# A linear-attention and expert layer on one core: the order of steps inside the token blocks is changed

## The chip, the core and the metric

The kernel runs on one core of a Trainium2 chip. The metric is the time of one execution on the device in microseconds (us); of several runs the median is taken. The engines named here are PE (TensorE), DVE (VectorE), ACT (ScalarE), POOL (GpSimd) and SP (SyncE, which here issues most DMAs).

## The reference

The input is x with 2 x 8192 tokens of 512 values. Two parts are added to it in turn.

```python
x = x + attention(layernorm(x))      # 16 heads of 32, chunks of 64 tokens
x = x + experts(layernorm(x))        # 64 experts, top 8, 256 places each, and a shared one

# attention: q, k, v are projections; alpha = 0.9 * sigmoid(silu(x Wg1 + bg1) Wg2 + bg2) + 0.1
scores = einsum('bhncd,bhnkd->bhnck', qc, kc) / sqrt(D)   # inside a chunk, causal
intra  = einsum('bhnck,bhnke->bhnce', softmax(scores), vc)
def step(S, inp):                                         # one token after the other
    q_t, k_t, v_t, a_t = inp
    inter_t = einsum('bhd,bhde->bhe', q_t, S)
    return a_t[..., None] * S + k_t[..., None] * v_t[..., None, :], inter_t
# experts: softmax of the router's logits, the best 8, their weights normed; an expert takes
# its first 256 tokens; silu(x Wg) * (x Wu) Wd; the shared expert has 384 hidden values
```

## The kernel before

There are two stages. `phase_tokens` goes through 64 blocks of 256 tokens and writes the attention's output with the shared expert added (`out_dram`), the normed rows with their router weights (`norm_rows`), and the counts of tokens by expert. `phase_experts` then goes through the 64 experts; the change does not touch it.

Every engine has its own program, and semaphores tie them together. In `phase_tokens` an engine's program is a loop over `step(t)`, where `t` is a block, `n` the next one and `m` the one after that. A step is a list of calls written out by hand, and that list is the order in which the engine works; an engine that has to wait holds all that stands behind. PE's steps work on three blocks at once: the end of block `t` (its last scores and outputs, the shared expert), the projections and first scores of `n`, and the transposes, the gate and half of the query projection of `m`. PE's loop body holds 16 steps and is run three times, then 14 steps follow written out, and a tail for the last two blocks.

What PE does in a block falls into two kinds.

Large products (`split_product`, L802 to L804): each product of float values is made of three, high by high, high by low, low by high. `project` makes keys and queries (12 products of 256 columns for each quarter, called a part), `values` and `down` have 512 columns, `gate_up` makes 24 products for each third of the hidden values.

Small products: `scores(t, u)` (four a block) has decayed keys by decayed queries (`inter`, L901) and queries by keys (`intra`, L915), one for each head and chunk. `outputs(t, u)` (four a block) has probabilities by values (L960) and the state by decayed queries (L972). `state_updates(t, odd)` (L881) has keys by values for the state, first the even chunks, then the odd ones; the second call waits for the first one's last product (`dk_filled`). The profile has two records for each of these products and one for each large one. So `scores` is 96 records of products, `outputs` 64, and `state_updates` 64, each with as many weight loads.

Between them stand transposes: `xt` (L819), `ktok` (L861), `turn_probs` (L938), `turn_out` (L983), `x2t` (L993), `turn_logits` (L1019).

Four of the eight banks of PSUM are shared by 23 jobs of PE. The table `JOBS` names for each job its bank and, in the order of its rows, what came in the bank before it; `take` (L790) lets PE wait for the reader of the last tenant.

POOL makes the inverse products (`unpair`, L494 and L496), folds them, and multiplies keys (`decayed_k`, L529) and queries (`decayed_q`, L521). `scores(n, 0)` waits for both, `ktok` for the keys. `rstd2(t, k)` (L473) gives DVE the factor that `norm2` waits for.

DVE reads scores and outputs from PSUM, makes the softmax, and has the scans of the decays (`decays`, L1278), the routing (`route_a`, `route_b`, `route_rows`), the state (`state`, chunk by chunk) and the sums. SP waits in a fixed order (L396 to L406): for both `x2_ready`, then it loads X of the block after next; for `rows_ready` (from `route_rows`), then it stores the normed rows; for `out_ready` (from `total`), then it stores the output; for the counts, then it stores these.

Of the kernel before, what the change touches and what calls it, by code (L numbers as in the profile page):

```python
# [135 lines left out]
def phase_tokens(nc, x_rows, Wq, bq, Wk, bk, Wv, bv, Wg1, bg1, Wg2, bg2, router_w, ws_gate_up,  # L136
                 ws_down, out_rows, norm_rows, counts_dram, ends_dram):
    ctx = ExitStack()
    with ctx:
# [284 lines left out]
        def _(pool):  # L424
# [123 lines left out]
            fold(Turn(0, 63))  # L548
            decayed_k(Turn(0, 63))
            decayed_q(Turn(0, 63))  # L550
# [5 lines left out]
        def _(act):  # L556
# [116 lines left out]
            def q_evac(t, k):  # L673

                qk_evac(t, k, q_filled, q_ready, QT, bq4s, SCALE, ("Qa", "Qb"))
# [5 lines left out]
            def step(t):  # L681
                n = t.next()
                m = t.next(2)
                q_evac(n, 0)
                gate2(n, 0)
# [27 lines left out]
                gate1(m)  # L713
                exp(n, 1)
                s1_high(m)
# [4 lines left out]
            gate1(Turn(0, 0))  # L720
            s1_high(Turn(0, 0))
            q_evac(Turn(0, 0), 0)
# [9 lines left out]
            exp(Turn(0, 0), 0)  # L732
            xt_evac(Turn(0, 1), 0)
            xt_evac(Turn(0, 1), 1)
            gate1(Turn(0, 1))
            exp(Turn(0, 0), 1)
            s1_high(Turn(0, 1))
# [3 lines left out]
            q_evac(Turn(0, 63), 0)  # L741
            gate2(Turn(0, 63), 0)
# [15 lines left out]
            ktok_evac(Turn(0, 63), 0)  # L758
            router_exp(Turn(0, 62))
            ktok_evac(Turn(0, 63), 1)  # L760
            hidden_high(Turn(0, 62), 0)
            gu(Turn(0, 62), 1)
            exp(Turn(0, 63), 0)
            hidden_high(Turn(0, 62), 1)
            gu(Turn(0, 62), 2)
            hidden_high(Turn(0, 62), 2)
# [20 lines left out]
        def _(pe):  # L787
# [1295 lines left out]
```

## Time and profile before

| what | us |
|---|---|
| median of 3 runs | 4517.09 |
| lowest and highest run | 4503.93, 4520.61 |
| the profiled execution, whole | 4525.55 |
| its span, first to last instruction | 4523.8 |
| PE busy | 4300.5 (95%) |
| PE weight loads busy | 3867.9 (86%) |
| DVE busy | 3486.0 (77%) |
| ACT busy | 2285.8 (51%) |
| POOL busy | 1326.0 (29%) |
| mean granted clock of PE | 0.967 |

The page is of one execution. Weight loads lie beside products, so both can be busy at once. Matmuls are pipelined and their ends are modelled: how far apart products start tells more than how long one takes. A clock of 1.00 is 2.4 GHz, 0.50 is 1.2 GHz. "issue" as a releaser means that the engine stood although nothing that the profile shows held it. The token stage fills the first 3565 us, the experts the rest.

### The profile page before, as it was taken

Reading aid. Unit: us, or ns where it says so; the run is one execution under the profiler, and the core shown is the slowest. Engines: PE = TensorE matmul, PEld = TensorE weight load, DVE = VectorE, ACT = ScalarE, POOL = GpSimd, SP = SyncE. Lnnn points to the kernel's source line nnn. Section 1 sums busy time; section 2 is a strip of 40 time slices with the busy share of each in tenths; the row PEclk is TensorE's granted clock in tenths of the full one; section 3 lists DMA queues with packets and bytes.
Section 4 is the critical chain, followed back from the end, with each engine's and each line's share of the span. In section 5 each row is a group of like instructions: output and inputs, shape, how many; then the busy total and the mean of one; then the engine's idle time right before and its main releaser. Section 6 shows DMA issues by size and latency. Waiting matters only on the chain. (4 is left out here: it accounts for less than half of the span.)

```text
span 4523.8 us, 182121 instructions
## 1 busy us (share of the span) xinstructions
PE 4300.5 (95%) x73868; PEld 3867.9 (86%) x73868; DVE 3486.0 (77%) x7674; ACT 2285.8 (51%) x7515; POOL 1326.0 (29%) x1266
## 2 busy tenths in 40 slices
PE   5999999999999999999999999999999689999998
PEld 4888888888888888888888888888888579999998
DVE  5777777777777777777777777777777588888887
ACT  4444444444445444444444444545444256666665
POOL 1222222222222222222222222222222156666665
PEclk9999999999999999999999999999999789999999
DMA  2010000000001001001011000110110179999997
GB/s 65 33 36 32 32 32 32 32 32 32 32 32 42 32 32 32 32 32 32 32 37 32 32 32 32 32 32 32 38 37 32 71 235 265 269 265 269 269 265 194
DMA packets 195679, 357.32 MB, mean 79 GB/s; under 512 B 17856, under 2 KB 94016, under 8 KB 194992
## 3 DMA queue, kind: packets, MB, share of 16 engines
q1 hardware_dynamic: 161488, 268.55, 17.7%
q0 software_dynamic: 33632, 79.73, 7.8%
q8 instruction: 544, 8.91, 0.8%
q14 instruction: 15, 0.12, 0.0%
HBM read 242.95 MB, written 107.50 MB: 77 GB/s over the span
## 5 line engine op out<-in xcount | busy, mean ns | idle before, releaser
L473 POOL TENSOR_TENSOR rs<-ve,neg_half 128x1 f32<-128x1 f32 x128 | 78.5, 614 | 2537.1 <-DVE ve L1377 2536.9
L618 ACT ACTIVATE PR<-PR,MX 128x64 f32<-128x64 f32 x2048 | 680.6, 337 | 2.0 <-DVE MX L1336 1.7
L802 PE MATMUL bank<-XBh,wsguh 128*128 128x256 f32 x1536 | 442.0, 288 | 1.5 <-DVE WG L1448 1.5
L626 ACT ACTIVATE OTs<-ot_bank 128x256 f32<-128x256 f32 x256 | 98.4, 384 | 677.6 <-PE ot_bank L960 677.4
L1936 PE MATMUL ebank<-XH,WH 128*128 128x256 f32 x1536 | 430.7, 280 | 7.6 <-DVE XL L2018 7.6
L803 PE MATMUL bank<-XBl,wsguh 128*128 128x256 f32 x1536 | 430.8, 280 | 0.0
L804 PE MATMUL bank<-XBh,wsgul 128*128 128x256 f32 x1536 | 430.8, 280 | 0.0
L1936 PE MATMUL ebank<-XH,WL 128*128 128x256 f32 x1536 | 429.6, 280 | 0.0
L1936 PE MATMUL ebank<-XL,WH 128*128 128x256 f32 x1536 | 429.6, 280 | 0.0
L618 ACT ACTIVATION_READ_ACCUMULATOR PR<-PR,MX 128x1 f32 x2048 | 389.6, 190 | 0.0
L2011 DVE TENSOR_TENSOR WL<-WS,WH 128x768 fp32r<-128x768 f32 (+1 forms) x455 | 370.9, 839 | 16.2
L802 PE MATMUL bank<-XTh,wkh 128*128 128x256 f32 x1024 | 338.9, 331 | 1.6 <-issue 1.1
L1873 ACT ACTIVATE WH<-WS 128x768 fp32r<-128x768 f32 (+1 forms) x455 | 325.2, 747 | 28.1 <-DMA WS<-in_L_ffn_w_down_dram 28.1
L803 PE MATMUL bank<-XTl,wkh 128*128 128x256 f32 x1024 | 312.5, 305 | 2.6 <-issue 2.6
L804 PE MATMUL bank<-XTh,wkl 128*128 128x256 f32 x1024 | 311.8, 304 | 2.0 <-issue 2.0
L802 PE MATMUL bank<-XTh,wqh 128*128 128x256 f32 x1024 | 299.3, 292 | 0.0
L1936 PEld LDWEIGHTS ebank<-XH,WH 128*128 128x128 f32 x1536 | 289.4, 188 | 11.1 <-issue 8.0
L802 PEld LDWEIGHTS bank<-XBh,wsguh 128*128 128x128 f32 x1536 | 290.0, 189 | 1.7 <-DVE WG L1448 1.6
L1936 PEld LDWEIGHTS ebank<-XL,WH 128*128 128x128 f32 x1536 | 288.6, 188 | 2.1
L803 PEld LDWEIGHTS bank<-XBl,wsguh 128*128 128x128 f32 x1536 | 290.3, 189 | 0.0
L804 PEld LDWEIGHTS bank<-XBh,wsgul 128*128 128x128 f32 x1536 | 289.9, 189 | 0.0
L1936 PEld LDWEIGHTS ebank<-XH,WL 128*128 128x128 f32 x1536 | 289.5, 189 | 0.0
(231 smaller groups left out, 13341.0 us busy)
## 6 DMA issues: line engine op xcount, KB each, us to landing
WS<-in_L_ffn_w_gate_dram SPq DMA_DIRECT2D x65, 768.0 KB
WS<-in_L_ffn_w_up_dram SPq DMA_DIRECT2D x65, 768.0 KB
WS<-in_L_ffn_w_down_dram SPq DMA_DIRECT2D x65, 768.0 KB
norm_rows<-XR SPq DMA_DIRECT2D x64, 576.0 KB, 3.9
X<-in_L_attn_x_dram SPq DMA_DIRECT2D x64, 512.0 KB, 3.6
out_dram<-X SPq DMA_DIRECT2D x64, 512.0 KB, 5.1
CR<-token_counts,count_at POOLq DMA_INDIRECT x136
XG<-norm_rows,row_at POOLq DMA_INDIRECT x132
```

The source lines that it names most:

```text
L473: nc.gpsimd.tensor_tensor(rs2[:, k:k + 1], ve2[:, k:k + 1], neg_half[:, k:k + 1], ALU.pow).then_inc(rstd2_ready.sem, 1)
L618: ins = nc.scalar.activation(PR[b][:, j, :], PR[b][:, j, :], ACT.Exp, bias=MX[b][:, j:j + 1], scale=1.0, accum_out=SU[b][:, j:j + 1])
L626: nc.scalar.activation(OTs[u // 2][:, 2 * (u % 2):2 * (u % 2) + 2, :], ot_bank[:, 0:2 * P].rearrange("p (a b) -> p a b", a=2), ACT.Copy).t ...
L802: nc.tensor.matmul(out, sh, mh, start=first, stop=False)
L803: nc.tensor.matmul(out, sh, ml, start=False, stop=False)
L804: return nc.tensor.matmul(out, sl, mh, start=False, stop=last)
L1873: nc.scalar.activation(WH[t.buf][:, cols], WS[t.buf][:, cols], ACT.Copy).then_inc(wh_ready.sem, 1)
L1936: last = nc.tensor.matmul(bank[HID[m]][:, a * CAP:(a + 1) * CAP], w, x[odd][:, c, :], start=(c == 0 and i == 0), stop=(c == KC - 1 and i = ...
L2011: v.tensor_tensor(WL[t.buf][:, cols], WS[t.buf][:, cols], WH[t.buf][:, cols].bitcast(f32), ALU.subtract).then_inc(wl_ready.sem, 1)
```

## The change

Only orders are changed, and with them the table of banks. On PE: `outputs(t, 0)` moves from behind `turn_probs(t, 1)` to the step before, between pieces of `down`; `scores(n, 2)` and the gate products move up; `scores(t, 3)` opens the step; halves of the key projection stand behind it and behind `outputs(t, 1)`; the two halves of the state products are parted by `xt`, the turn of the normed rows; `scores(n, 0)` comes ahead of `ktok(n, 0)`; some pieces of `values`, of the query projection and of `x2t` are joined. On POOL the queries come ahead of the keys and `unpair` ahead of `rstd2(t, 0)`. On ACT and DVE some 20 steps move by a few places; on DVE `route_rows` goes ahead of `scores_part(n, 1)`, the scans move from the head of a step to the end of the one before, ahead of `total(t, 1)`, and `state` is called in three pieces where it was two. The opening and the tail, written out by hand, are changed in the same way.

```diff
 JOBS = {
-    "Ka": (2, 1), "Kb": (0, 1), "ATr0": (1, 0), "Qb": (3, 1), "V0": (1, 1), "V1": (0, 1), "ATr1": (2, 0), "X2Ta": (3, 0),
-    "X2Tb": (2, 0), "RL": (3, 0), "GU0": (2, 0), "RLT": (3, 0), "KTok0": (0, 1), "KTok1": (0, 1), "GU1": (2, 0), "DK": (0, 1),
...
+    "Ka": (2, 1), "ATr0": (1, 0), "Kb": (0, 1), "Qb": (3, 1), "V0": (1, 1), "ATr1": (2, 0), "V1": (0, 1), "X2Ta": (3, 0),
+    "X2Tb": (2, 0), "RL": (3, 0), "GU0": (1, 0), "RLT": (3, 0), "KTok0": (2, 1), "KTok1": (3, 1), "GU1": (0, 0), "DK": (1, 1),
...
             def step(t):
                 n = t.next()
                 fold(t)
+                decayed_q(t)
                 decayed_k(t)
-                decayed_q(t)
                 rstd1(n)
+                unpair(n)
                 rstd2(t, 0)
-                unpair(n)
                 rstd2(t, 1)
 
             rstd1(Turn(0, 0))
...
             def step(t):
                 n = t.next()
                 m = t.next(2)
-                q_evac(n, 0)
-                gate2(n, 0)
                 gate2(n, 1)
                 alpha(n)
                 ot(t, 0)
@@ -699,27 +697,29 @@
                 lt(t)
                 gu(t, 0)
                 ktok_evac(n, 0)
+                ktok_evac(n, 1)
                 router_exp(t)
-                ktok_evac(n, 1)
+                hidden_high(t, 0)
                 normalise(m)
-                hidden_high(t, 0)
                 gu(t, 1)
+                xt_evac(m, 0)
+                hidden_high(t, 1)
+                xt_evac(m, 1)
+                gu(t, 2)
                 exp(n, 0)
-                xt_evac(m, 0)
-                xt_evac(m, 1)
-                hidden_high(t, 1)
-                gu(t, 2)
+                gate1(m)
                 hidden_high(t, 2)
-                gate1(m)
+                q_evac(m, 0)
+                s1_high(m)
                 exp(n, 1)
-                s1_high(m)
+                gate2(m, 0)
 
...
             def step(t):
                 n = t.next()
                 m = t.next(2)
-                turn_probs(t, 1)
+                scores(t, 3)
                 project(n, 0, wk, k_filled, ("Ka", "Kb"), parts=(0,))
-                outputs(t, 0)
-                scores(t, 3)
                 outputs(t, 1)
-                project(n, 1, wk, k_filled, ("Ka", "Kb"), parts=(0,))
-                turn_out(t, 0)
                 project(n, 0, wk, k_filled, ("Ka", "Kb"), parts=(1,))
                 turn_probs(t, 2)
-                project(n, 1, wk, k_filled, ("Ka", "Kb"), parts=(1,))
+                turn_out(t, 0)
+                project(n, 1, wk, k_filled, ("Ka", "Kb"), parts=(0,))
+                project(n, 1, wq, q_filled, ("Qa", "Qb"), parts=(0,))
                 outputs(t, 2)
                 turn_probs(t, 3)
-                project(n, 1, wq, q_filled, ("Qa", "Qb"), parts=(0,))
+                project(n, 1, wk, k_filled, ("Ka", "Kb"), parts=(1,))
+                outputs(t, 3)
                 values(n, 0, chunks=(0,))
-                outputs(t, 3)
-                values(n, 1, chunks=(0,))
                 turn_out(t, 1)
-                values(n, 1, chunks=(1,))
                 project(n, 1, wq, q_filled, ("Qa", "Qb"), parts=(1,))
+                values(n, 1, chunks=(0, 1))
                 values(n, 0, chunks=(1, 2))
                 x2t(t, 0)
+                x2t(t, 1)
                 values(n, 1, chunks=(2,))
-                x2t(t, 1)
                 values(n, 0, chunks=(3,))
                 values(n, 1, chunks=(3,))
                 router_high(t)
                 router_low(t)
                 gate_up(t, 0)
                 turn_logits(t)
+                scores(n, 0)
                 ktok(n, 0)
-                scores(n, 0)
                 ktok(n, 1)
                 gate_up(t, 1)
                 state_updates(n, 0)
-                state_updates(n, 1)
                 xt(m, 0)
                 xt(m, 1)
+                state_updates(n, 1)
+                positions(t)
                 gate_up(t, 2)
                 scores(n, 1)
-                positions(t)
                 gate1(m)
-                turn_probs(n, 0)
                 project(m, 0, wq, q_filled, ("Qa", "Qb"))
                 down(t, 0, (0, 1))
+                turn_probs(n, 0)
+                scores(n, 2)
+                gate2(m, 0)
+                gate2(m, 1)
                 down(t, 0, (2,))
+                outputs(n, 0)
                 down(t, 1, (0, 1))
                 down(t, 1, (2,))
-                gate2(m, 0)
-                gate2(m, 1)
-                scores(n, 2)
+                turn_probs(n, 1)
 
...
             def step(t):
                 n = t.next()
                 m = t.next(2)
-                decays(n)
-                scores_part(t, 3)
                 softmax_b(t, 2)
                 products(n)
+                decay_part(t, 3)
+                weights(t, 2)
                 residual(t, 0)
-                weights(t, 2)
-                decay_part(t, 3)
                 softmax_b(t, 3)
+                inverse(n, 0)
+                weights(t, 3)
+                inverse(n, 1)
                 variance2(t, 0)
-                weights(t, 3)
-                inverse(n, 0)
-                inverse(n, 1)
                 residual(t, 1)
                 variance2(t, 1)
                 norm2(t, 0)
...
                 route_b(t)
                 hidden_low(t, 0)
                 hidden(t, 1)
-                state(n, (0,))
                 xt_low(m, 0)
+                state(n, (0, 1))
                 xt_low(m, 1)
+                route_rows(t)
+                scores_part(n, 1)
                 hidden_low(t, 1)
                 hidden(t, 2)
+                state(n, (2,))
+                silu1(m)
                 softmax_b(n, 0)
-                scores_part(n, 1)
-                state(n, (1, 2, 3))
-                silu1(m)
+                decay_part(n, 1)
+                state(n, (3,))
                 hidden_low(t, 2)
+                s1_low(m)
                 route_c(t)
-                decay_part(n, 1)
                 weights(n, 0)
+                scores_part(n, 2)
+                decay_part(n, 2)
                 total(t, 0)
-                s1_low(m)
                 softmax_b(n, 1)
-                route_rows(t)
+                decays(m)
+                weights(n, 1)
                 total(t, 1)
-                scores_part(n, 2)
-                weights(n, 1)
-                decay_part(n, 2)
+                scores_part(n, 3)
 
...
```

What follows are rows of the built programs, PE first, of one block in the middle of PE's loop, without register instructions where dots stand. A row names line, operation, written and read tiles, the size and how many follow each other; one small product here is two records in the profile. First PE before, from the first outputs of a block to its second ones (L960 and L972 are `outputs`, L901 and L915 `scores`):

```order
L960 MATMUL ot_bank<-WT,V 32x64 x8
L972 MATMUL ot_bank<-QD,R 32x64 x16
L960 MATMUL ot_bank<-WT,V 32x64 x8
L901 MATMUL sa<-QD,RI 32x64 x2
...
L915 MATMUL sa<-KT,QT 64x64 x16
...
L901 MATMUL sa<-QD,RI 32x32 x2
L960 MATMUL ot_bank<-WT,V 32x64 x8
L972 MATMUL ot_bank<-QD,R 32x64 x16
```

PE after, from the first outputs of a block to its second ones (`wsd` is the shared expert's second matrix, `wk` the keys'):

```order
L835 MATMUL bank<-sg,wg 128x256 x2
L802 MATMUL bank<-wsdh,HTh 128x512
L803 MATMUL bank<-wsdl,HTh 128x512
L804 MATMUL bank<-wsdh,HTl 128x512
L960 MATMUL ot_bank<-WT,V 32x64 x8
L972 MATMUL ot_bank<-QD,R 32x64 x16
...
L938 MATMUL pt_bank<-ident,PR 128x128 x4
L901 MATMUL sa<-QD,RI 32x64 x2
...
L915 MATMUL sa<-KT,QT 64x64 x16
...
L802 MATMUL bank<-XTh,wkh 128x256
...
L960 MATMUL ot_bank<-WT,V 32x64 x8
```

First outputs, fourth scores and second outputs stood in one run; now three blocks of large products, 3, 9 and 12, lie ahead of each of the three.

PE before, at the state products (L881) and the turn of the normed rows of the block after (L819):

```order
L804 MATMUL bank<-XBh,wsgul 128x256
L881 MATMUL bank<-V,KTok 32x32 x64
...
L819 MATMUL sa<-ident,XN 128x128 x4
L819 MATMUL pt_bank<-ident,XN 128x128 x4
L802 MATMUL bank<-XBh,wsguh 128x256
```

PE after, at the same place (L1028 is `positions`):

```order
L881 MATMUL bank<-V,KTok 32x32 x32
...
L819 MATMUL sa<-ident,XN 128x128 x4
L819 MATMUL pt_bank<-ident,XN 128x128 x4
L881 MATMUL bank<-V,KTok 32x32 x32
L1028 MATMUL ot_bank<-upto,M 64x256
```

The eight transposes went between the halves, and `positions` came up behind them.

POOL before, one step (L502 to L510 fold, L469 is `rstd1`, L473 `rstd2`):

```order
L510 TENSOR_TENSOR AL<-AL,r_mid 128x16x32
...
L529 TENSOR_TENSOR RI<-KT,RI 128x1024
L518 REGISTER_ALU
L521 TENSOR_TENSOR QD<-QT,AL 128x1024
L468 REGISTER_ALU
L469 TENSOR_TENSOR rs<-ve,neg_half 128x2
L472 REGISTER_ALU
L473 TENSOR_TENSOR rs<-ve,neg_half 128x1
L492 REGISTER_ALU
L494 TENSOR_TENSOR RI<-PV,AL 128x32x16
L496 TENSOR_TENSOR RI<-PV,AL 128x32x16
```

POOL after, the same step:

```order
L521 TENSOR_TENSOR QD<-QT,AL 128x1024
L527 REGISTER_ALU
L529 TENSOR_TENSOR RI<-KT,RI 128x1024
L468 REGISTER_ALU
L469 TENSOR_TENSOR rs<-ve,neg_half 128x2
L492 REGISTER_ALU
L494 TENSOR_TENSOR RI<-PV,AL 128x32x16
L496 TENSOR_TENSOR RI<-PV,AL 128x32x16
L472 REGISTER_ALU
L473 TENSOR_TENSOR rs<-ve,neg_half 128x1 x2
```

Queries and keys changed places, and both calls of `rstd2` now stand behind `unpair`.

## Rows read from the trace of the kernel before

**Rows 1.** The page: busy time, share of the span and instructions of each engine.
```profile
PE 4300.5 (95%) x73868; PEld 3867.9 (86%) x73868; DVE 3486.0 (77%) x7674; ACT 2285.8 (51%) x7515; POOL 1326.0 (29%) x1266
```

**Rows 2.** Line 835 in the token stage: duration least/median/most, first and last start.
```profile
L835 PE MATMUL bank<-sg,wg x252: 274/280/356, 89.8 to 3494.8; 128*128 128x256 f32 x126
```

**Rows 3.** Stretches of one block: length, busy time of engines, clock, DMA share, GB/s.
```profile
2181.33:2236.22 54.89, 53.72 (x1058) 47.70 (x1057) 42.11 (x97) 26.36 (x100) 11.23 (x10) 0.97 0.09 33
2236.22:2292.77 56.55, 54.49 (x1058) 48.54 (x1057) 42.07 (x97) 26.34 (x100) 11.48 (x10) 0.94 0.10 32
2791.40:2844.00 52.60, 52.07 (x1058) 46.22 (x1058) 42.12 (x97) 26.35 (x100) 11.50 (x10) 1.00 0.10 34
...
3331.10:3383.80 52.70, 52.19 (x1058) 46.32 (x1058) 42.17 (x97) 26.36 (x100) 11.51 (x10) 1.00 0.10 34
```

**Rows 4.** Waits of PE, 140 to 3440: line, releaser, us in total, times, longest.
```profile
PE ot_bank L960 <- issue: 25.5, 18, 2.9
PE sa L901 <- issue: 18.3, 15, 1.6
PE bank L881 <- PE bank L881: 16.2, 60, 0.4
PE ot_bank L972 <- issue: 13.9, 10, 1.8
PE sa L915 <- issue: 7.8, 12, 0.9
PE pt_bank L938 <- issue: 6.9, 2, 3.7
```

**Rows 5.** Timeline of PE: start, duration, instructions; in brackets the idle time before.
```profile
2238.99 0.28 PE L802 MATMUL bank<-XTh,wkh 128*128 128x256 f32 x1
2239.11 0.28 PE L803 MATMUL bank<-XTl,wkh 128*128 128x256 f32 x1
...
2241.44 0.44 PE L901 MATMUL sa<-QD,RI 32*32 32x64 f32 x32
2241.80 0.69 PE L915 MATMUL sa<-KT,QT 32*64 32x64 f32 x32
...
2245.35 0.85 PE L972 MATMUL ot_bank<-QD,R 32*32 32x64 f32 x21 [1.79 <-issue]
...
2247.10 0.41 PE L803 MATMUL bank<-XTl,wkh 128*128 128x256 f32 x1
2247.31 0.41 PE L804 MATMUL bank<-XTh,wkl 128*128 128x256 f32 x1
```

**Rows 6.** A stretch with its DMA share; a store's issue on SP; the instruction queue.
```profile
2238.60:2242.40 3.80, 3.80 (x142) 3.26 (x140) 3.77 (x7) 1.54 (x5) 0.00 (x0) 1.00 0.80 296
...
2238.29 1.80 SPq L404 DMA_DIRECT2D out_dram<-X  x1
...
q8 instruction: 544, 8.91, 0.8%
```

**Rows 7.** A stretch behind the stall.
```profile
2244.80:2246.00 1.20, 0.65 (x21) 0.61 (x20) 1.17 (x5) 0.00 (x0) 0.00 (x0) 0.50 0.00 0
```

**Rows 8.** The first of three long stretches of the token stage.
```profile
189.00:1279.00 1090.00, 1056.20 (x20822) 939.50 (x20822) 832.05 (x1891) 519.25 (x1973) 224.78 (x199) 0.97 0.10 33
```

**Rows 9.** Timeline of DVE at the scans.
```profile
2240.87 2.49 DVE L1278 TENSOR_TENSOR_SCAN AL<-AL,seg_start 128x264 f32<-128x264 f32 x4
```

**Rows 10.** Timeline of PE at the state products.
```profile
2220.68 0.68 PE L881 MATMUL bank<-V,KTok 64*32 64x32 f32 x56 [0.27 <-PE bank L881]
...
2221.81 0.63 PE L819 MATMUL sa<-ident,XN 128*128 128x128 f32 x4
```

**Rows 11.** Timeline of POOL at the queries.
```profile
2211.20 2.22 POOL L521 TENSOR_TENSOR QD<-QT,AL 128x1024 f32<-128x1024 f32 x1
```

**Rows 12.** Timeline of PE at the first scores.
```profile
2214.32 0.61 PE L861 MATMUL bank<-ident,RI 128*128 128x128 f32 x4
2214.86 0.44 PE L901 MATMUL sa<-QD,RI 32*32 32x64 f32 x32
```

More of the change, by code:

```diff
@@ L720, in _ @@
             gate1(Turn(0, 0))
+            q_evac(Turn(0, 0), 0)
             s1_high(Turn(0, 0))
-            q_evac(Turn(0, 0), 0)
             gate2(Turn(0, 0), 0)
@@ L1128, in _ @@
             values(Turn(0, 0), 1, chunks=(3,))
+            scores(Turn(0, 0), 0)
             ktok(Turn(0, 0), 0)
-            scores(Turn(0, 0), 0)
             ktok(Turn(0, 0), 1)
             state_updates(Turn(0, 0), 0)
-            state_updates(Turn(0, 0), 1)
             xt(Turn(0, 1), 0)
             xt(Turn(0, 1), 1)
+            state_updates(Turn(0, 0), 1)
             scores(Turn(0, 0), 1)
             gate1(Turn(0, 1))
+            project(Turn(0, 1), 0, wq, q_filled, ("Qa", "Qb"))
             turn_probs(Turn(0, 0), 0)
-            project(Turn(0, 1), 0, wq, q_filled, ("Qa", "Qb"))
+            scores(Turn(0, 0), 2)
             gate2(Turn(0, 1), 0)
             gate2(Turn(0, 1), 1)
-            scores(Turn(0, 0), 2)
+            outputs(Turn(0, 0), 0)
+            turn_probs(Turn(0, 0), 1)
             with nc.Fori(0, 24, 8, engines=[pe.engine], hint_back_edge=True) as pair:
@@ L1176, in _ @@
             turn_logits(Turn(0, 62))
+            scores(Turn(0, 63), 0)
             ktok(Turn(0, 63), 0)
-            scores(Turn(0, 63), 0)
             ktok(Turn(0, 63), 1)
@@ L1182, in _ @@
             state_updates(Turn(0, 63), 1)
+            positions(Turn(0, 62))
             gate_up(Turn(0, 62), 2)
             scores(Turn(0, 63), 1)
-            positions(Turn(0, 62))
+            down(Turn(0, 62), 0, (0, 1))
             turn_probs(Turn(0, 63), 0)
-            down(Turn(0, 62), 0, (0, 1))
+            scores(Turn(0, 63), 2)
             down(Turn(0, 62), 0, (2,))
+            outputs(Turn(0, 63), 0)
             down(Turn(0, 62), 1, (0, 1))
             down(Turn(0, 62), 1, (2,))
-            scores(Turn(0, 63), 2)
             turn_probs(Turn(0, 63), 1)
-            outputs(Turn(0, 63), 0)
             scores(Turn(0, 63), 3)
             outputs(Turn(0, 63), 1)
+            turn_probs(Turn(0, 63), 2)
             turn_out(Turn(0, 63), 0)
-            turn_probs(Turn(0, 63), 2)
             outputs(Turn(0, 63), 2)
@@ L1208, in _ @@
             gate_up(Turn(0, 63), 1)
+            positions(Turn(0, 63))
             gate_up(Turn(0, 63), 2)
-            positions(Turn(0, 63))
             down(Turn(0, 63), 0, (0, 1))
@@ L1548, in _ @@
             decay_part(Turn(0, 0), 0)
-            state(Turn(0, 0), (0,))
             xt_low(Turn(0, 1), 0)
+            state(Turn(0, 0), (0, 1))
             xt_low(Turn(0, 1), 1)
+            scores_part(Turn(0, 0), 1)
+            state(Turn(0, 0), (2,))
+            silu1(Turn(0, 1))
             softmax_b(Turn(0, 0), 0)
-            scores_part(Turn(0, 0), 1)
-            state(Turn(0, 0), (1, 2, 3))
-            silu1(Turn(0, 1))
             decay_part(Turn(0, 0), 1)
+            state(Turn(0, 0), (3,))
+            s1_low(Turn(0, 1))
             weights(Turn(0, 0), 0)
-            s1_low(Turn(0, 1))
+            scores_part(Turn(0, 0), 2)
+            decay_part(Turn(0, 0), 2)
             softmax_b(Turn(0, 0), 1)
-            scores_part(Turn(0, 0), 2)
+            decays(Turn(0, 1))
             weights(Turn(0, 0), 1)
-            decay_part(Turn(0, 0), 2)
+            scores_part(Turn(0, 0), 3)
             START = links[0]
@@ L1569, in _ @@
             links[0], links[1] = START + 62 * LINKS, None
-            decays(Turn(0, 63))
-            scores_part(Turn(0, 62), 3)
             softmax_b(Turn(0, 62), 2)
             products(Turn(0, 63))
+            decay_part(Turn(0, 62), 3)
+            weights(Turn(0, 62), 2)
             residual(Turn(0, 62), 0)
-            weights(Turn(0, 62), 2)
-            decay_part(Turn(0, 62), 3)
             softmax_b(Turn(0, 62), 3)
+            inverse(Turn(0, 63), 0)
+            weights(Turn(0, 62), 3)
+            inverse(Turn(0, 63), 1)
             variance2(Turn(0, 62), 0)
-            weights(Turn(0, 62), 3)
-            inverse(Turn(0, 63), 0)
-            inverse(Turn(0, 63), 1)
             residual(Turn(0, 62), 1)
@@ L1632, in _ @@
             hidden(Turn(0, 63), 1)
+            route_rows(Turn(0, 63))
             hidden_low(Turn(0, 63), 1)
@@ L1637, in _ @@
             total(Turn(0, 63), 0)
-            route_rows(Turn(0, 63))
             total(Turn(0, 63), 1)
```

63 lines of the change are left out of this document (30 added, 33 removed), and 2 rows, old and new, of the table JOBS.

## The prediction

> **What bounds the kernel now.** I began with the shares on the page [rows 1]: PE is busy 95% of the span, DVE 77%, ACT 51%, POOL 29%. The expert stage is untouched, so the question is how long PE takes for the 64 blocks of the token stage. Line 835 runs in fours, once a block: 252 records, 63 fours, from 89.8 to 3494.8 us [rows 2], and (3494.8 - 89.8) / 62 = 54.9 us a block.
>
> Next I asked for stretches that are single blocks [rows 3], because a block whose PE never idles tells the floor. Two blocks take 52.60 and 52.70 us, both at clock 1.00. One of 54.89 us has a mean clock of 0.97 and one of 56.55 us has 0.94. DVE and ACT are busy for the same 42 and 26 us in all of them, so neither sets the difference.
>
> Then the waits of PE alone, over some 60 blocks [rows 4]. Hardly any name another engine. The large ones are "issue", the engine having nothing that it waits for by the profile: L960 25.5, L901 18.3, L972 13.9, L915 7.8, L938 6.9, in sum 72.4 us. Beside them stands L881 waiting for L881, 16.2 us in 60 times: that is the second half of the state products, which waits for the last product of the first half.
>
> The timeline shows where "issue" falls [rows 5]. From 2240.14 on come 224 small products with no large one between (records of L960, L972, L960, then L901, L915, L901, then L960, L972, L960: 64 + 96 + 64), and in the third group PE stands for 1.79 us. Small products run at 0.37 us for 32 (2241.44 to 2241.80), large ones at 0.12 us each: PE eats its instructions ten times as fast here. Meanwhile, from 2238.6 to 2242.4, the DMA engines are 80% busy and move 296 GB/s, 1.1 MB, which is the store of normed rows (576 KB) and that of the output (512 KB) together [rows 6]. Instructions come by DMA too: 544 packets, 8.91 MB, 16.4 KB each [rows 6]. With 2 x 73868 PE instructions [rows 1] that is at most some 270 of them a packet, 135 products with their weight loads. The run of 224 always crosses such a border, in about 2.4 us for 135 products where the block's mean (1056 products) would be 7 us. My reading: the next packet of instructions comes too late, and the stores make it later.
>
> Behind the stall the granted clock is 0.50 [rows 7], that is 1.2 instead of 2.4 GHz. Products of 256 columns then start 0.21 us apart instead of 0.12 [rows 5]. Three stretches of 1090 us, from 189 to 3459, all have a mean clock of 0.97 [rows 8], so the half clock holds for 6% of 3270 us, 196 us.
>
> **The change part by part.** No arithmetic is added or removed; every term is an order.
>
> PE, second products. `outputs(t, 0)` goes ahead by some 5 us, between the pieces of `down`, and a half of the key projection (12 products) stands between `scores(t, 3)` and `outputs(t, 1)`. The run of 224 becomes 64, 96 and 64, with large products between: 3 of 512 columns ahead of `outputs(t, 0)` and 9 behind it (2.1 us, taken as twice 0.12 each), and 12 of 256 columns (1.4 us) ahead of `outputs(t, 1)`. 135 products from the start of `scores(t, 3)` then take the 96 small ones (1.36 us), 12 large ones (1.4 to 1.5 us) and 27 small ones (0.6 us): 3.4 us instead of 2.4.
>
> DVE and SP, the stores. `route_rows` moves ahead of `scores_part(n, 1)`, so the store of normed rows (576 KB) leaves some 10 us sooner, in or before the 24 large products of `gate_up(t, 2)`. The other store (512 KB) waits for `total(t, 1)`, which now stands behind the four scans, 2.49 us [rows 9]; it leaves 2 to 4 us later, alone. The burst beside the small products is halved.
>
> What these two give: the floor is read from the fast blocks. 54.9 - 52.65 = 2.25 us, times 62 = 140 us for both the stalls and the clock. As a check, 72.4 us of stalls and (0.21 - 0.12) / 0.21 = 43% of 196 us = 84 us of clock make 156; they overlap, so I stay with 140. Of it some 15 us stay: PE's loop jumps back twice and leaves once, and I read the longest waits as these (L938 twice, 6.9 us in all, L960 once 2.9 us), with some 5 us of clock behind them. Of the other 125 I take 85%, 106 us, since `scores(n, 2)` and `outputs(n, 0)` are only four small gate products and three large ones apart and a stretch there may still stall. The bounds are 0 (the stalls have another cause) and 125.
>
> The Trainium skill speaks against this term. Its page "Runtime: NRT & Kernel Launch", section "Instruction fetch mechanics", has blocks of 16 KiB (256 instructions) fetched while the current one runs, hidden because the sequencer dispatches more slowly than they come. The size agrees with the packets here; that it is always hidden does not agree with 72.4 us of "issue" among the small products. By the rule this term would be 0 and only the next one would stand.
>
> PE, state products. The eight transposes of the normed rows go between the two halves of L881. They take 2221.81 to 2222.63, 0.8 us [rows 10], and the wait that they cover is 0.27 us. It goes whole: 17 us over 64 blocks. The bounds are 0 and 17. What is late next there is `positions`, now ahead of `gate_up(t, 2)` (3 us sooner): it needs the last step of DVE's `route_b`, and its risk is counted with the rest below.
>
> POOL. The query product now comes ahead of the key product, and `scores(n, 0)` ahead of `ktok(n, 0)`. The scores need both, so they wait for the second, which ends at 2211.20 + 2.22 = 2213.42 as before [rows 11]. They start where `ktok` does, 2214.32 instead of 2214.86 [rows 12]: 0.9 us of slack, cost 0. `unpair` now stands ahead of `rstd2(t, 0)`: that wait holds `norm2(t, 0)` and so `x2t`, and it can cost something if POOL's 2.4 us there (two products of 1.2 us) come late. The bounds are 0 and 1 us a block, 62 us; I take 0, since norm2 of both tiles now follows variance2 of both, and `x2t` stands right behind them only after 9 products of 512 columns.
>
> The rest. The DVE, ACT and bank tables move many steps by 1 to 3 us. Each PE job waits for the reader of its bank. On PE the changes of kind (small, large, transpose) number 35 a block before and after, so the border cost of 0.1 us is the same. PE's slack on the other engines is about 0.5 us or more where I could lay the steps side by side: I take 0, with 0 and 0.5 us a block (31 us) as bounds. Prologue and tail change by single steps: 0, within 3 us.
>
> **Sum.** 106 + 17 = 123 us. From the profiled execution, 4525.6 us (span 4523.8), that leaves 4403. The median of the timed runs is 4517.1, 8.5 below the profiled one, so I say 4395 us.
>
> **The rivals.**
> The stall follows the store (14%). The 512 KB store now leaves about when `scores(t, 3)` starts, and 96 + 64 small products with 1.4 us between may still run dry. For: the DMA engines were busy in just this place. Against: half the bytes, and 3.4 us instead of 2.4. I give it 35% of the 125 us, 44, and the 17: 4456.
> A wait on another engine takes the place (13%). Most likely are the softmax products of DVE before `turn_probs(t, 2)`, or norm2 behind `unpair`. At 0.5 us a block it takes 31 us back: 4426. For: DVE is busy 42 of 53 us [rows 3] and its steps are pressed together. Against: PE has nearly no such wait now, in any block.
> The stall has nothing to do with the run (5%). Only the 17 us come: 4500. For: blocks differ (52.6 to 56.6 us) at the same order. Against: five lines of small products hold nearly all of "issue".
> The clock falls more often (3%). Small products now lie at two more places, and if each of them brings the half clock for 3.4 us more, a block loses 2 x 1.5 us: 62 x 3 = 186 us, less 64 us of stalls and 17 us of waits gained: 4622. It is slower from 2.3 us a block on. For: the clock falls where small products stand. Against: the 128 state products in 1.7 us pass at clock 1.00 now in the fast blocks.
> My forecast has 65%.
>
> **How the numbers follow.** Faster by over 0.5% (23 us, about the least that a measurement of this kernel tells from no change): forecast, first and second rival, 92%. Within: most of the third, 5%. Slower: 3%. The range: at the low end all 125 + 17 us, 4375, and 15 us for the spread of the runs (4503.9 to 4520.6), 4360; at the high end it takes in the first rival, 4465.
>
> **What would show it.** In the profile after: waits of PE for "issue" under 25 us in these lines; L881 waiting for L881 gone; mean clock of the token stage 0.99; blocks of 52.3 to 53.3 us; a norm_rows store issued about 10 us ahead of the out store. I am wrong if "issue" stays near 72 us, if the clock stays at 0.97 without it, or if PE shows waits for DVE, ACT or POOL of over 0.3 us in each block.

## The result

The kernel after takes 4373.32 us in the median of four runs (4368.55 to 4378.76), the kernel before 4518.85 us in the runs beside them (4503.93 to 4526.28). The ratio is 0.9679, with a 95% interval of 0.9661 to 0.9697: 145.5 us less. The prediction said 4395 us, in a range of 4360 to 4465. The profiled execution took 4374.81 us, its span 4373.1 us.

The page of the kernel after, answering to [rows 1]:

```profile
PE 4239.3 (97%) x73868; PEld 3804.2 (87%) x73868; DVE 3481.6 (80%) x7674; ACT 2285.9 (52%) x7515; POOL 1339.1 (31%) x1266
```

The instructions are the same in number. PE is busy 61 us less for the same products, which start further apart at 1.2 GHz; the other 90 us of the 151 that the span lost were idle time. The group of L835, as in [rows 2]:

```profile
L835 PE MATMUL bank<-sg,wg x256: 277/281/387, 52.5 to 3347.7; 128*128 128x256 f32 x128
```

Before, the first group that the trace held began at 89.8 us and the last at 3494.8 us; after, the last begins at 3347.7. The gain is in the token stage.

Stretches of the kernel after (length, busy time of PE, PEld, DVE, ACT, POOL, clock, DMA share, GB/s): a block like most, the block behind a jump of PE's loop, and the long stretch of [rows 8]:

```profile
1039.50:1091.70 52.20, 52.20 (x1061) 46.27 (x1057) 41.93 (x97) 26.45 (x102) 11.22 (x10) 1.00 0.10 35
929.10:986.30 57.20, 55.06 (x1064) 48.68 (x1056) 41.97 (x97) 26.40 (x102) 11.23 (x10) 0.94 0.09 32
...
189.00:1279.00 1090.00, 1086.81 (x21821) 962.63 (x21811) 873.14 (x1984) 547.35 (x2086) 237.79 (x209) 1.00 0.11 35
```

In the first row PE is busy for all of its 52.20 us. Taken from L835 to L835 the middle one of 59 blocks now has 52.18 us; the fastest of [rows 3] had 52.60. The clock of the long stretch went from 0.97 to 1.00. The second row is one of three exceptions, told below.

The waits of PE over the same window as [rows 4], 140 to 3440 (line, releaser, us in total, times, longest):

```profile
PE sa L901 <- issue: 9.4, 9, 2.1
PE bank L802 <- DVE WG L1445: 4.3, 2, 2.9
PE bank L993 <- DVE XR L1381: 2.5, 1, 2.5
PE ot_bank L960 <- DVE WT L1359: 1.3, 2, 0.9
```

"issue" falls from 72.4 us in the five largest lines (79.6 us in all nine) to 9.4 in one (9.8 with one short wait at L802), and L881 waiting for L881 is gone. The rows for DVE come once or twice each, behind 3280 us, at the end of the stage. None repeats by the block.

The timeline of PE in the kernel after, where [rows 5] show the stall (start, duration, instructions; in brackets the idle time before):

```profile
991.90 0.44 PE L901 MATMUL sa<-QD,RI 32*32 32x64 f32 x32
992.27 0.69 PE L915 MATMUL sa<-KT,QT 32*64 32x64 f32 x32
992.89 0.44 PE L901 MATMUL sa<-QD,RI 32*32 32x64 f32 x28
993.85 0.25 PE L901 MATMUL sa<-QD,RI 32*32 32x32 f32 x4 [0.52 <-issue]
994.03 0.38 PE L802 MATMUL bank<-XTh,wkh 128*128 128x256 f32 x1
...
995.63 0.43 PE L960 MATMUL ot_bank<-WT,V 64*32 64x64 f32 x16
995.99 0.65 PE L972 MATMUL ot_bank<-QD,R 32*32 32x64 f32 x32
```

This is one of the nine stalls that are left, 0.52 us at the 93rd record of a run of 96. The next 12 large products give room, and the second outputs pass without a gap. Six of the nine lie in the blocks at PE's loop jumps or right behind them.

The state products (L881), the transposes between them (L819) and `positions` (L1028), as in [rows 10]:

```profile
1024.81 0.76 PE L881 MATMUL bank<-V,KTok 64*32 64x32 f32 x64
1025.52 0.64 PE L819 MATMUL sa<-ident,XN 128*128 128x128 f32 x4
...
1026.52 0.76 PE L881 MATMUL bank<-V,KTok 64*32 64x32 f32 x64
1027.21 0.30 PE L1028 MATMUL ot_bank<-upto,M 128*64 128x256 bf16 x1
```

No brackets: PE waits for nothing here. The stores on SP's queue, as in [rows 6]:

```profile
2236.51 0.37 SPq L402 DMA_DIRECT2D norm_rows<-XR  x1
2252.76 0.37 SPq L404 DMA_DIRECT2D out_dram<-X  x1
```

They leave 16.2 us apart, where they left 0.6 us apart before.

### The profile page after: what moved, and what is told of

It reads as the page before. It is cut to its first block and busy times, and to the rows that moved or that the text cites. A ratio compares the mean times of both kernels' runs of the same rounds, so it can differ in the third digit from the quotient of the medians.

```text
span 4373.1 us, 182288 instructions
## 1 busy us (share of the span) xinstructions
PE 4239.3 (97%) x73868; PEld 3804.2 (87%) x73868; DVE 3481.6 (80%) x7674; ACT 2285.9 (52%) x7515; POOL 1339.1 (31%) x1266
## 5 line engine op out<-in xcount | busy, mean ns | idle before, releaser
L494 POOL TENSOR_TENSOR RI<-PV,AL 128x512 f32<-128x512 f32 x64 | 77.6, 1213 | 2562.9 <-DVE PV L1287 2562.9
L802 PE MATMUL bank<-XBh,wsguh 128*128 128x256 f32 x1536 | 443.4, 289 | 0.0
L2011 DVE TENSOR_TENSOR WL<-WS,WH 128x768 fp32r<-128x768 f32 (+1 forms) x455 | 370.4, 838 | 16.2
L802 PE MATMUL bank<-XTh,wkh 128*128 128x256 f32 x1024 | 313.9, 307 | 0.4 <-issue 0.4
L802 PEld LDWEIGHTS bank<-XBh,wsguh 128*128 128x128 f32 x1536 | 289.6, 189 | 9.3
L1359 DVE TENSOR_TENSOR WT<-pt_bank,AM 128x512 f32<-128x512 f32 x256 | 175.8, 687 | 149.7 <-PE pt_bank L938 55.6
L802 PE MATMUL bank<-XTh,wqh 128*128 128x256 f32 x1024 | 293.2, 286 | 0.0
L804 PE MATMUL bank<-XTh,wkl 128*128 128x256 f32 x1024 | 290.2, 283 | 0.0
```

The source lines that it names most:

```text
L494: nc.gpsimd.tensor_tensor(inverse[:, :, 0:half], PV[:, :, :], running[:, :, HC:half:-1], ALU.mult).then_inc(folded.sem, 1)
L802: nc.tensor.matmul(out, sh, mh, start=first, stop=False)
L804: return nc.tensor.matmul(out, sl, mh, start=False, stop=last)
L1359: v.tensor_tensor(WT[u % 2][:, :, :], pt_bank[:, :].rearrange("p (n k) -> p n k", k=P), AM[u % 2][:, :, :], ALU.add).then_inc(w_ready.sem, 1)
L2011: v.tensor_tensor(WL[t.buf][:, cols], WS[t.buf][:, cols], WH[t.buf][:, cols].bitcast(f32), ALU.subtract).then_inc(wl_ready.sem, 1)
```

## The experiments

My theory (the recorded expectations call it theory S): the run of 224 small products outruns the delivery of PE's instructions; each stall can be followed by a time at 1.2 GHz; the state products' wait is a second term of its own. The rivals: the stall comes from the burst of stores, from PE's loop, or the gain comes from the orders of the other engines. Intervals are 95%; a ratio is to the kernel before in the same runs. Waits are over 140 to 3440 us for kernels as slow as before, over 140 to 3280 for the faster ones, whose token stage ends sooner.

### One part alone, from the kernel before

**e1**, half of the key projection between the fourth scores and the second outputs:

```diff
                 scores(t, 3)
-                outputs(t, 1)
                 project(n, 1, wk, k_filled, ("Ka", "Kb"), parts=(0,))
+                outputs(t, 1)
```

> The kernel before, with one half of the key projection (12 products) moved from behind the second outputs to between the fourth scores and the second outputs; nothing else is changed. Theory S (PE runs out of instructions where small products follow each other for too long, and the stores beside them make it worse): the run of 224 small products becomes 160, 12 large ones, 64. Part of the issue stalls goes; the run of 160 still lies beside the stores, so I expect 72 us of issue waits to fall to 20 to 45 and the time to 4440 to 4480. Theory B (only the burst of the two stores matters, not the run): no change, 4505 to 4525. Theory O (the stalls have another cause): no change either, and the stall keeps its place behind the same count of products.

Measured: 4487.3 us (4486.24 to 4493.02), ratio 0.9946 (0.9926 to 0.9965), 7 us above the range that my theory gave. Waits of PE:

```profile
PE bank L983 <- ACT OTs L626: 36.3, 61, 0.6
PE sa L901 <- issue: 20.1, 16, 1.7
PE bank L881 <- PE bank L881: 16.0, 60, 0.3
PE pt_bank L938 <- issue: 7.2, 2, 3.7
```

The stalls of L972 are gone, as the cut should do, and "issue" is 46 us in all its lines. But `turn_out` now stands right behind `outputs(t, 1)` and waits 0.6 us in each block for ACT's evacuation. The time fell by 31 us by the medians (24 by the ratio). So the cut is worth 31 + 36 = 67 us at most here, and more than half goes back into a new wait. The change has `turn_out` a step later.

**e2**, the state products alone:

```diff
                 state_updates(n, 0)
-                state_updates(n, 1)
                 xt(m, 0)
                 xt(m, 1)
+                state_updates(n, 1)
```

> The kernel before, with the eight transposes of the normed rows put between the two halves of the state products. The wait of L881 for L881 (16 us over 60 blocks) goes. If that wait is worth its full length, the time falls by 15 to 17 us, to 4500 to 4503; the issue stalls and the clock stay as they are. A rival: the second half then fills later, state and all of DVE behind it come later, and nothing is gained (4510 to 4525).

Measured: 4497.13 us (4490.99 to 4507.97), ratio 0.9957 (0.9943 to 0.9971). The wait of L881 is gone and the stalls are as before:

```profile
PE ot_bank L960 <- issue: 25.9, 18, 3.8
PE sa L901 <- issue: 19.8, 15, 1.6
PE ot_bank L972 <- issue: 14.0, 11, 1.8
```

**e3**, the store of normed rows earlier: `route_rows(t)` from ahead of `total(t, 1)` to behind `xt_low(m, 1)`, nothing else.

> The kernel before, with DVE's route_rows moved up behind xt_low(m, 1), so that the store of the normed rows (576 KB) leaves some 12 us ahead of that of the output (512 KB). Theory S: the burst beside the run of 224 is halved, the run stays; a third to two thirds of the stalls go, time 4430 to 4490. Theory B: nearly all stalls and the half clock go, 4370 to 4410. Theory O: no change.

Measured: 4470.48 us (4466.72 to 4477.8), ratio 0.991 (0.989 to 0.9931), 40 us less. Waits:

```profile
PE ot_bank L960 <- issue: 22.5, 18, 3.9
PE bank L881 <- PE bank L881: 16.3, 61, 0.3
...
PE sa L901 <- issue: 9.7, 17, 1.2
...
PE sa L915 <- issue: 1.6, 6, 0.4
```

PE stalls at the same places, mostly for less time: L901 9.7 instead of 18.3 us, L915 1.6 instead of 7.8. In all lines "issue" is 65 us, 14 less than before. The clock makes up more than this: a block has 1.56 us at 1.2 GHz on average, where it had 3.01.

### One part undone, from the kernel after

**e4**, `route_rows(t)` back to just ahead of `total(t, 1)`.

> The kernel after, with DVE's route_rows moved back to just ahead of total(t, 1), so that both stores leave together again, with the short runs of small products kept. Theory S: the runs are short, so a few stalls return where the burst lies, 4380 to 4410 against 4373. Theory B: all stalls return, 4480 to 4510. Theory O: no change.

Measured: 4372.22 us (4371.89 to 4379.99), ratio 0.9687 (0.967 to 0.9704): nothing, where my theory wanted 7 us or more. With the runs short, the two stores together cost no time.

**e5**, the key half behind the second outputs again, so that the runs are 64 and 160:

```diff
                 scores(t, 3)
-                project(n, 0, wk, k_filled, ("Ka", "Kb"), parts=(0,))
                 outputs(t, 1)
+                project(n, 0, wk, k_filled, ("Ka", "Kb"), parts=(0,))
```

> The kernel after, with the half of the key projection moved from between the fourth scores and the second outputs to behind these: runs of 64 and 160 small products instead of 64, 96 and 64. Theory S: 160 is long enough to run dry when a border of the instruction stream lies in it, so 10 to 30 us of issue waits return and the time is 4390 to 4430. A rival (the stores decide, and they are now apart): 4370 to 4380.

Measured: 4397.76 us (4394.2 to 4399.23), ratio 0.9744 (0.9714 to 0.9774), 24 us over the kernel after. Of these, 10 us are a new wait for DVE. Waits:

```profile
PE ot_bank L960 <- DVE WT L1359: 10.4, 42, 0.3
PE sa L901 <- issue: 9.2, 8, 2.1
PE ot_bank L960 <- issue: 5.1, 8, 2.1
```

**e6**, the first outputs behind `turn_probs(n, 1)` again, so that the runs are 160 and 64:

```diff
                 down(t, 0, (2,))
-                outputs(n, 0)
                 down(t, 1, (0, 1))
                 down(t, 1, (2,))
                 turn_probs(n, 1)
+                outputs(n, 0)
```

> The kernel after, with the first outputs moved from between the pieces of the shared expert's second product to just ahead of the fourth scores: runs of 160 and 64. Theory S: the same as for the other run of 160, 4390 to 4430. The rival that only the stores decide: 4370 to 4380.

Measured: 4440.74 us (4438.95 to 4447.16), ratio 0.9846 (0.9815 to 0.9877), 67 us over, and 11 us above the range of my theory. Of these, 19 us are a new wait for DVE, which my theory did not have. Waits:

```profile
PE sa L901 <- issue: 25.7, 20, 3.5
PE pt_bank L938 <- DVE PR L1349: 19.2, 59, 0.4
PE sa L915 <- issue: 8.0, 8, 1.3
```

**e9**, the edits of e5 and e6 together: the run of 224 is whole again, all else is as in the kernel after.

> The kernel after with both moves taken back, so that first outputs, fourth scores and second outputs stand in one run of 224 small products, as before; the stores stay apart and all other orders of the kernel after stay. Theory S: some 50 to 60 us of issue waits and 40 to 70 us of half clock return, 4430 to 4470. If the other orders (DVE, POOL, banks, stores) made the gain: 4370 to 4390.

Measured: 4524.06 us (4506.56 to 4539.92, one execution of 8105.56 us aside), ratio 1.0017 (0.9996 to 1.0038): the whole gain is gone, 54 us more than the upper end of my range. Waits, and PE's timeline in one block:

```profile
PE sa L901 <- issue: 21.6, 20, 2.9
PE pt_bank L938 <- DVE PR L1349: 19.8, 61, 0.4
PE ot_bank L972 <- issue: 14.9, 13, 1.6
PE ot_bank L960 <- issue: 13.4, 13, 1.7
PE sa L915 <- issue: 8.5, 8, 1.5
```

```profile
1354.19 0.43 PE L960 MATMUL ot_bank<-WT,V 64*32 64x64 f32 x16
1354.55 0.53 PE L972 MATMUL ot_bank<-QD,R 32*32 32x64 f32 x22
1356.48 0.41 PE L972 MATMUL ot_bank<-QD,R 32*32 32x64 f32 x10 [1.39 <-issue]
```

This is the stall of [rows 5] again, at the same line, in a kernel whose stores are apart and whose state products are parted. Three terms make up most of the difference to the kernel after: 51 us more of "issue" in all lines (60.9 less 9.8), 73 us of clock (2.95 us a block at 1.2 GHz instead of 0.23, counted as below), and 20 us of a wait for DVE, since `turn_probs(n, 1)` has lost the small outputs that covered its wait. These 20 us do not come from the length of the run, so about 130 of the 151 us are what the whole run costs.

The two halves of the cut are not additive. Undone one by one they cost 24.4 and 67.4 us, which make 92; undone together they cost 151. Seen from e9, the first outputs moved alone (this is e5) give 126 us and the key half moved alone (this is e6) gives 83.

**e10**, e9 with `route_rows(t)` back as in e4.

> The kernel after, with its small products again in one run of 224, and the store of norm_rows again issued at its old place, beside that run. The kernel with the run of 224 and the store apart took 4524.06 us, with low clock in 39 of 59 blocks. My theory, that the store lengthens the instruction stalls only where the run is long (40 us before, nothing in the kernel after): 4545 to 4580 us, more than 25 us of further stalls or low clock. The rival, that the 40 us of the store in the kernel before came from one particular coincidence of the store with one instruction fetch, which this order does not have: 4515 to 4535 us, the same as with the store apart.

Measured: 4523.12 us (4514.22 to 4534.54), ratio 1.0013 (0.9995 to 1.0032), the same as e9. The stores do leave together, inside a block's run:

```profile
1369.93 0.37 SPq L402 DMA_DIRECT2D norm_rows<-XR  x1
1370.53 0.37 SPq L404 DMA_DIRECT2D out_dram<-X  x1
```

My theory fell here: it wanted 25 us or more. The 40 us of e3 were seen only in the order of the kernel before.

**e7**, GpSimd's order of before (`decayed_k` ahead of `decayed_q`, `rstd2(t, 0)` ahead of `unpair(n)`).

> The kernel after, with GpSimd's order alone put back to that of before (decayed_k ahead of decayed_q, and the reciprocals ahead of unpair, as before). My theory, that GpSimd's and VectorE's orders carry none of the gain and that they only have to stay off TensorE's path: 4370 to 4380 us, blocks of 52.2 us, no new wait of TensorE on GpSimd. The rival, that GpSimd's new order is needed because the new TensorE order wants decayed_q or the reciprocals earlier: a wait of some tenths of a us in each of the 62 blocks, 0.3 to 1 us x 62 = 19 to 62 us more, 4392 to 4435 us.

Measured: 4371.97 us (4371.48 to 4379.56), ratio 0.9692 (0.9663 to 0.9721). The only wait of PE that is over 1 us is the L901 one of the kernel after:

```profile
PE sa L901 <- issue: 8.8, 7, 2.4
```

**e11**, the state products joined again.

> The kernel after, with the two halves of the state products again behind each other, without the turn of the normed rows between them. My theory, that the wait of the second half for the accumulation of the first is 0.27 us in each block and independent of the stalls: 4373.3 + 0.27 x 62 = 4390 us (4386 to 4392), and TensorE's wait at L881 on L881 back at 16 us. The rival, that the wait is hidden once the stalls are gone: 4373 us.

Measured: 4393.57 us (4391.74 to 4399.32), ratio 0.9738 (0.9709 to 0.9767), 20 us over the kernel after. The wait is back, 0.27 us a time:

```profile
PE bank L881 <- PE bank L881: 15.8, 59, 0.4
```

### The loop

**e8** is the kernel after and **e12** the kernel before, each with PE's 62 steps written out:

```diff
-            with nc.Fori(0, 24, 8, engines=[pe.engine], hint_back_edge=True) as pair:
-                for odd in range(16):
-                    step(Turn(pair, odd))
-            for odd in range(48, 62):
+            for odd in range(62):
                 step(Turn(0, odd))
```

> The kernel after, with PE's loop of 16 steps written out for all 62 steps, so that PE's program has no jump in the token stage; order and work are the same. In the kernel after, the blocks behind the three passes of the loop take 57.2, 55.7 and 56.1 us and those following 53.1 to 53.5 where 52.2 is normal, 15 to 16 us in sum. If the jump costs this, the time is 4356 to 4360. If a longer program costs as much elsewhere (its instructions are fetched anyway), 4370 to 4376.

> The kernel before, with TensorE's loop over the blocks written out for all 62 steps and nothing else changed. My theory, that the stalls come from the run of 224 small products and not from the loop: the stalls for instructions stay (more than 55 of 72 us), low clock stays in over 30 of 59 blocks, and only the 8 us of the three jumps go: 4505 to 4515 us. The rival, that the instruction fetch falls behind because of the loop's buffer or its branch: stalls below 20 us, blocks of 52.5 us, 4380 to 4420 us.

Measured: e8 4365.83 us (4364.9 to 4369.28), ratio 0.9675 (0.9646 to 0.9704); e12 4504.45 us (4482.76 to 4509.51), ratio 0.9971 (0.9954 to 0.9988). The waits of e8, then of e12:

```profile
PE sa L901 <- issue: 3.6, 6, 0.8
```

```profile
PE ot_bank L972 <- issue: 21.0, 16, 1.9
PE sa L901 <- issue: 19.2, 16, 1.6
PE ot_bank L960 <- issue: 18.4, 15, 1.7
PE bank L881 <- PE bank L881: 16.6, 61, 0.5
```

Without a loop the kernel before still stalls for 68 us in all lines (79.6 with the loop), and this profiled execution was the fastest of its ten: the loop is not the cause of most of the stalls. By the ratio it gains 13 us. What the loop costs is seen in the kernel after, in the block from 929.1 to 986.3 above, behind a jump back:

```profile
937.05 0.32 PE L901 MATMUL sa<-QD,RI 32*32 32x32 f32 x4 [2.13 <-issue]
937.30 1.00 PE L915 MATMUL sa<-KT,QT 32*64 32x64 f32 x25
```

The L915 group takes 1.00 us for 25 records where 0.69 us did for 32: the granted clock is 0.50 there. Three such blocks (57.24, 55.65 and 56.07 us, behind the two jumps back and the loop's end) lie 12.4 us over 52.18 in sum, with the blocks behind them 15.6 us. e8 has none of them; the largest of its 59 blocks has 53.4 us. It is 7.5 us below the kernel after in the median, half of the 15.6, since its usual block has 52.25 us instead of 52.18, 4 us over the stage. Its 4365.83 us lie between the two ranges that I had named. It is the fastest kernel here, by a margin that the two ratios alone do not establish.

## Why the prediction was right, and where its sizes were off

**The run of 224.** This was the main step, and e9 shows it from the one side and the kernel after from the other: with the run whole 4524 us, with it cut 4373 us, all other orders equal; some 20 us of this are a wait for DVE. The burst of stores (e4, e10), the loop (e12) and POOL's order (e7) are excluded as the cause of what was gained.

That the stalls are waits for instructions I had only argued, from the length of the run and the size of the packets. The trace shows it. It has each packet of the instruction queue with its time; the one ahead of the stall in [rows 5], over 2242.8 to 2243.2:

```profile
q8 instruction: 1, 0.02, 14.4%
```

This packet starts at 2242.93 us and ends at 2243.85; the one before it ended at 2239.69. PE stands from 2243.56 and goes on at 2245.35, 1.50 us behind the end of the packet. In the 59 blocks from 145 to 3384 us PE stalls 68 times for "issue", and all 68 stalls end 1.2 to 1.8 us behind the end of the last packet; of moments taken at random, 11% lie so. In e12 it is 64 stalls of 64, in e9 57 of 59. A packet comes for every 254 records of products and weight loads. What makes a packet start when it does, no run here shows.

How a stall becomes more than its own length can be counted from the traces. Blocks of the kernels before and e9, sorted by how long the granted clock stood at 1.2 GHz in them (mean length, mean of the sum of "issue" stalls):

| at 1.2 GHz | before | e9 |
|---|---|---|
| not at all | 21 blocks, 53.3 us, 0.9 us | 20 blocks, 53.0 us, 0.5 us |
| 3.4 us | 28 blocks, 55.1 us, 1.4 us | 27 blocks, 55.2 us, 1.1 us |
| 6.8 us | 7 blocks, 56.7 us, 1.5 us | 12 blocks, 57.2 us, 1.6 us |
| more | 3 blocks, 60.0 us, 3.4 us | none |

From the first row to the second the stalls grow by 0.4 to 0.6 us and the block by 1.9 to 2.1 us: the other 1.5 us is the lower clock (43% of 3.4 us, as [rows 5] had it). After, only the three blocks at the loop's jumps have time at 1.2 GHz. A block has 3.01 us of it before and 0.23 after, which is (3.01 - 0.23) x 0.43 x 62 = 74 us. With 70 us of stalls (79.6 - 9.8) and 16 us of L881 that makes an estimate of 160 us, against 150.7 between the two profiled executions. Dearer products in the new order, told next, take 10 to 30 us of it back, so the count closes to within some 20 us.

**The size of this term.** I had capped it at 140 us, left 15 at the loop and taken 85% of the rest, 106. Two sizes were off, both too low. The floor: I read 52.65 us from the fastest blocks, but these still held small stalls beside the 0.27 us of L881, and the new blocks take 52.18. So (54.89 - 52.18) x 62 = 168 us stood open, state products included, where I had 140 + 17 = 157. That is 11 us. And the 85%: I feared that `scores(n, 2)` and `outputs(n, 0)`, with seven large products between, would still stall. They do not. "issue" stands in nine places only, at L901. Those 19 us came too. 11 + 19 = 30 us is about what lies between the 4403 us that I had for the profiled execution and its 4374.8 us.

But 52.18 us is the floor of the new order and not of the old one. In e3, whose PE has the order of before, eleven blocks have no stall for "issue"; without the wait at L881 they take 51.7 to 52.0 us. So the same products take 0.2 to 0.5 us a block longer in the new order, 10 to 30 us over the stage; at `turn_probs` (L938) it is 1.90 us a block instead of 1.54. I had put this cost at the borders between kinds of products at nothing, from a count of the changes. More than 168 us stood open, then, and the new order gave a part of it back. That these two came close to cancelling is luck.

**The loop jumps.** I had 15 us staying. They are 15.6. I had read them at L938 and L960 in the kernel before; after, all three are at L901, in the small products right behind the jump.

**The rule of the Trainium skill.** By the Trainium skill, "Runtime: NRT & Kernel Launch", section "Instruction fetch mechanics", which has the crossing of an instruction block "mostly hidden", this term would have been about 0. The runs decide against it for this kernel: e9 and the kernel after hold the same instructions in the same number and differ by 151 us, some 120 of it "issue" and the clock.

**State products.** 17 us predicted; e2 gives 19 (by its ratio), e11 gives 20, the waits 16. The difference to 16 us is below what I can place. It costs about the same with the stalls and without, so the two terms look independent. The wait is one that the program itself sets: the second half waits for the semaphore of the first one's last product.

**The stores.** I said that they make the late packet later, and gave them no number of their own in the sum. e3 shows 40 us in the kernel before; e4 and e10 show none in the other order, e10 even with the run whole. So the burst is not a cost by itself. In the kernel before the stores leave 2.4 us ahead of the run's first product (2182.8 and 2185.3 in the block before that of [rows 5]), in e10 3.7 us behind it (1369.9 and 1366.2); that this decides is only argued. Nor do the single terms add up: from e9's parted state products and stores apart I would have expected 4518 - 20 - 40 + 20 for the wait on DVE, 4478 us, and it took 4524. What makes up these 46 us stays open. My words that the stores make the packet later hold, if at all, for the order of before alone; the kernel after owes them nothing that a run shows. This does not touch the comparison of e9 with the kernel after.

**POOL and the rest.** Both at 0, and 0 was right: e7 is the kernel after to within 2 us, and no wait of PE for another engine repeats by the block. e1, e5 and e6 show how near such waits were. Each takes one of the moves away from the others, and PE waits at once for ACT (0.6 us a block), DVE (0.3) or DVE (0.3). The rival of a wait on another engine had 13%; it fails because the moves were made together: `turn_out` later, the outputs ahead of `turn_probs(n, 1)`, the key half ahead of the outputs.

**The clock.** The rival in which it falls more often had 3%. It did not: the small products at two more places passed at clock 1.00, 0.99 in the last third, which holds the loop's end and the tail. In this rival I had the kernel slower from 2.3 us a block on, which sets all 142 us that could be gained against the loss; by the 64 + 17 us of the rival's own sum it would be from 1.3 us on.

Of what was to be seen in the profile, most came: "issue" 9.4 us (under 25), L881 gone, the clock 1.00 (0.99), no wait by the block. Two readings missed: the blocks are just below the 52.3 to 53.3 us that I gave, and the stores are 16 us apart instead of 10.

## What to carry to other kernels

When an engine shows "issue" among its shortest instructions, count how many of them follow one another, and put long instructions between: here 96 in a row with 9 to 12 large products around them hardly stall, and 224 cost some 130 us. The cost is not additive in the cuts: from e9, either cut alone gave more than half of what both gave (126 and 83 of 151 us), while e1, one cut in the order of before, gave 31 us since a new wait took the rest. So the pieces must go where they also cover the waits for other engines. Read the floor from blocks in which the engine never stood, not from the fastest block, which may still hold the stall in question; and expect that a new order has a floor of its own.

## What the runs showed of the hardware

- PE stalls for its own instructions, 79.6 us of 4524 here, mostly in runs whose records start 12 to 23 ns apart. Each of the 68 stalls counted ends 1.2 to 1.8 us behind the end of a packet of the instruction queue. PE stalls in code written out as it does in a loop (68 us in e12).
- In the kernel after, the blocks at PE's two jumps back and at the loop's end, with those behind them, are about 5 us longer each: 1.8 to 2.1 us without instructions, then 3.4 or 6.8 us at 1.2 GHz, and up to 1.3 us in the block behind. The stall comes not at the jump itself but 5 to 28 records into the small products behind it. Written out (e8), the median is 7.5 us less.
- Each of the 38 times that the granted clock fell in these 59 blocks of the kernel before, a stall of 0.7 to 3.7 us was under way or had ended at most 2 us before. A block with 3.4 us at 1.2 GHz lost some 1.5 us by the clock, as much as its stalls took.
- The second half of the state products waited 0.27 us for the semaphore of the first half's last product (15.8 us in 59 times in e11), and 0.8 us of transposes between hide it whole.
